# Two of the shared expert's eight groups moved from the prelude to the head of the bridge, normalisation in quarters

## The chip, the cores and the metric

The kernel runs on one core of a Trainium2 chip. Times are device microseconds (us) of one execution. TensorE (PE) multiplies matrices into PSUM, VectorE (DVE), ScalarE (ACT) and GpSimd (POOL) work element by element, SyncE (SP) issues most of the transfers between HBM and SBUF. Everything is float32.

## What is computed

Two layers on 4096 tokens of width 256. Each adds to the stream a mixer and a mixture of experts, both fed by the same layer norm:

```python
xn = _layernorm(x)
x = x + _L0_attn_ref(xn, ...) + _L0_ffn_ref(xn, ...)   # state-space mixer; 16 experts, 4 a token
xn = _layernorm(x)
x = x + _L1_attn_ref(xn, ...) + _L1_ffn_ref(xn, ...)   # linear attention; 8 experts, 2 a token
...
def _L0_ffn_ref(...):
    ...
    shared = _swiglu(x, w1_s, w3_s, w2_s)              # silu(x @ w1.T) * (x @ w3.T) @ w2.T, hidden width 256
    return routed + shared
```

The change is about `shared`, the expert of layer 0 that every token goes through. It needs only layer 0's `xn`, and its result is needed when the stream of layer 0 is complete.

## The kernel before

Tokens come in 32 tiles of 128, and four tiles make a group (`NG` = 8 groups of 512). The program is a row of stages, each a block in which every engine has its own list of instructions; all engines meet between blocks. Within a block they wait for each other through semaphores alone, so the order of a list is what the source writes.

- **Norm phase** (`norm_phase`): loads x in four transfers of eight tiles, computes mean and variance (`moments`) in `PARTS` = 2 halves, ScalarE takes the root (`root`), VectorE writes `xn` of a group and SP stores it to `xn_rows`; TensorE turns it and ScalarE keeps it as `xnT` (column-wise, in SBUF until layer 1 overwrites it group by group). In steps 4 to 7 VectorE waits for the store of the group four before. ScalarE's list also issues the fill `blank` of the 18.6 MB slot buffer, after the second root.
- **Route phase** (`route_phase` with `decay_work` and `Shared`): VectorE computes the mixer's decay (`dt`), then the ranking of experts (`sel`), then, from the count of tokens per expert, the slots. TensorE runs the shared expert in 16 units (`up(j)`: gate and value of half the hidden width of a group) and 8 `down(g)`; before unit `SUMS` = 8 it makes the running sums of `dt` in two halves, and after unit `COUNT` - 1 = 13 the count. ScalarE copies out (`keep_up`, `keep_down`), POOL multiplies, SP stores each group to `shared_rows`. `keep_down(g)` from the third group on waits for the store of the group two before.
- **SSD stage**: the mixer proper, 179 to 1407 us.
- **First expert stage**, with `Join` beside it: per group it loads x, the mixer's output and `shared_rows`, POOL adds the bias, VectorE adds all up in `xs`.
- **Bridge** (`bridge_phase`, layer 1's block): POOL sums each token's four expert rows pairwise (`b_work`, loaded by SP in halves of a group), VectorE adds them to `xs`, normalises a group (one step per group), TensorE turns it and projects q, k and v; then routing and attention. A load for group g + 2 waits for VectorE's add of group g.
- **Second expert stage**, to the end.

## Time and profile before

| | |
|---|---|
| median of 3 runs | 2404.99 us (2403.39 to 2406.26) |
| the profiled execution, its own time | 2406.89 us |
| its span, first to last instruction | 2405.1 us |
| mean granted TensorE clock | 0.969 |
| TensorE busy in the span | 2187.2 us (91%) |
| VectorE, ScalarE, POOL busy | 1595.0, 1190.7, 1435.2 us |
| prelude (norm and route phase) | 0 to 179.3 us |
| SSD stage, first expert stage | 179.3 to 1407.3 to 1693.8 us |
| bridge, second expert stage | 1693.8 to 1963.5 to 2405.1 us |

A busy engine is not one at its peak. What a change is worth is read from the stage in which it sits: who is idle there, and what ended the wait. A granted clock of 1.00 is 2.4 GHz, one of 0.50 is 1.2 GHz.

### The profile page before, as it was taken

How to read it: one execution, taken by the hardware profiler on the slowest of the kernel's cores; microseconds unless marked ns; L12 is line 12 of the kernel's file. 1: busy time of each engine (PE TensorE's matmuls, PEld its weight loads, DVE VectorE, ACT ScalarE, POOL GpSimd, SP SyncE). 2: the span in 40 equal slices, each digit the busy share in tenths (PEclk: the TensorE clock that was granted, in tenths of full speed). 3: DMA queues.
4: the chain of work that ended last, by engine and by line, in shares of the span. 5: the costliest groups of instructions: out<-in, count | busy, mean ns of one | idle time of the engine just before them, and what ended most of it. 6: DMA issues, size and time to landing. Idle time of an engine off the chain costs nothing. (4 is left out here: it accounts for less than half of the span.)

```text
span 2405.1 us, 40728 instructions
## 1 busy us (share of the span) xinstructions
PE 2187.2 (91%) x12292; PEld 1586.7 (66%) x12292; DVE 1595.0 (66%) x3484; ACT 1190.7 (50%) x2677; POOL 1435.2 (60%) x1278
## 2 busy tenths in 40 slices
PE   4787999999999999999999989999288879999997
PEld 2455777777777777777777767777144656666665
DVE  4747888888888888888888845666687742222222
ACT  2356777777777777777777722222132341111111
POOL 1224777777777777777777756777643214444443
PEclk9898999999999999999999999999689899999999
DMA  7926454545545455454544448664540046222221
GB/s 255 359 83 146 139 151 132 152 139 151 149 132 156 136 154 145 133 156 139 153 143 132 141 139 278 191 218 150 202 157 1 1 166 173 46 44 45 45 43 20
DMA packets 195651, 330.34 MB, mean 137 GB/s; under 512 B 49267, under 2 KB 137588, under 8 KB 195188
## 3 DMA queue, kind: packets, MB, share of 16 engines
q1 hardware_dynamic: 139044, 233.43, 32.8%
q0 software_dynamic: 26880, 53.64, 8.8%
q10 hardware_dynamic: 29520, 40.66, 5.4%
q8 instruction: 110, 1.80, 0.3%
q14 instruction: 97, 0.79, 0.1%
HBM read 240.72 MB, written 87.84 MB: 137 GB/s over the span
## 5 line engine op out<-in xcount | busy, mean ns | idle before, releaser
L1006 DVE SCALAR_TENSOR_TENSOR m_cv<-m_hp,conv,m_cv 128x256 f32<-128x256 f32 x864 | 417.0, 483 | 112.2 <-ACT m_cv L905 91.0
L1397 PE MATMUL e_u<-wup,e_xgT 128*128 x1152 | 421.4, 499 | 9.0 <-issue 4.9
L1335 ACT ACTIVATE e_sil<-e_u 128x128 f32<-128x128 f32 (+1 forms) x216 | 82.9, 384 | 551.5 <-PE e_u L1397 524.5
L832 POOL TENSOR_TENSOR m_er<-m_er,m_cT 128x1024 f32<-128x1024 f32 x128 | 302.2, 2361 | 44.1 <-DVE m_ar L1013 44.1
L943 ACT ACTIVATE m_ar<-m_ar,m_ta 128x128 f32<-128x128 f32 x1024 | 318.7, 390 | 0.8
L1094 PE MATMUL m_hp<-xnT,wpj 128*128 128x259 f32 x1152 | 304.3, 387 | 7.8 <-PEq L144 4.5
L1397 PEld LDWEIGHTS e_u<-wup,e_xgT 128*128 128x128 f32 x1152 | 203.1, 191 | 141.3 <-issue 130.3
L1102 PE MATMUL m_gp<-xnT,wpj 128*128 128x256 f32 x1024 | 269.1, 385 | 11.2 <-ACT m_gT L923 11.2
L1094 PEld LDWEIGHTS m_hp<-xnT,wpj 128*128 128x128 f32 x1152 | 214.2, 192 | 68.8 <-issue 27.1
L1292 POOL DMA_INDIRECT out<-e_y,target x72 | 113.0, 1570 | 228.7 <-DVE e_y L1366 192.9
L839 POOL TENSOR_TENSOR m_hdd<-m_hdt,m_tb 128x512 f32<-128x512 f32 x128 | 131.0, 1043 | 193.8 <-DVE m_hdt L1021 193.8
L1153 PE MATMUL m_out<-wo,m_gT 128*128 128x256 f32 x1024 | 242.9, 380 | 0.0
L923 ACT ACTIVATE m_gT<-m_gp,bias 128x256 f32<-128x256 f32 x256 | 121.2, 473 | 232.3 <-PE m_gp L1102 189.2
L1153 PEld LDWEIGHTS m_out<-wo,m_gT 128*128 128x128 f32 x1024 | 193.0, 190 | 47.8 <-issue 23.9
L1414 PE MATMUL e_d<-wdn,e_hidT 128*128 x864 | 222.9, 381 | 1.0 <-DVE e_y L1366 1.0
L1359 DVE SCALAR_TENSOR_TENSOR e_hid<-e_sil,gate,e_u 128x512 f32<-128x512 f32 x72 | 53.8, 747 | 254.6 <-ACT e_sil L1335 240.5
L1102 PEld LDWEIGHTS m_gp<-xnT,wpj 128*128 128x128 f32 x1024 | 178.6, 191 | 35.9 <-ACT m_gT L923 19.1
L1300 POOL DMA_INDIRECT y_rows<-e_y,e_target x144 | 149.4, 1037 | 73.4 <-DVE e_y L1366 64.4
L873 POOL DMA_INDIRECT rows_by_slot<-m_xrow,posi x128 | 172.5, 1347 | 32.8 <-issue 26.5
L905 ACT ACTIVATE m_cv<-m_hp,m_bsum,conv 128x256 f32<-128x256 f32 x288 | 159.9, 555 | 53.9 <-PE m_hp L1094 51.3
L1414 PEld LDWEIGHTS e_d<-wdn,e_hidT 128*128 128x128 f32 x864 | 147.3, 190 | 23.4 <-issue 1.8
L1039 DVE SCALAR_TENSOR_TENSOR m_y<-m_hT,dcol,m_yt 128x128 f32<-128x128 f32 x512 | 143.2, 343 | 23.5 <-PE m_yt L1142 23.5
(305 smaller groups left out, 3965.8 us busy)
## 6 DMA issues: line engine op xcount, KB each, us to landing
m_ar<-acum_rows_dram SPq DMA_DIRECT2D x512, 128.0 KB
m_er<-eacum_rows_dram SPq DMA_DIRECT2D x128, 512.0 KB
rows_by_slot<-blank_rows ACTq DMA_DIRECT2D x1, 18576.0 KB, 79.1
e_xg<-rows_by_slot ACTq DMA_DIRECT2D x132, 129.0 KB
m_xrow<-xn_rows SPq DMA_DIRECT2D x32, 512.0 KB
b_work<-y_rows SPq DMA_DIRECT2D x16, 1024.0 KB, 7.0
wup<-in_w SPq DMA_DIRECT2D x8, 1024.0 KB
wpj<-in_w_proj SPq DMA_DIRECT2D x1, 4352.0 KB, 24.4
```

Source lines behind the costliest of these rows:

```text
L832: g.tensor_tensor(er[:, t], er[:, t], middle(cT[:, t * P:(t + 1) * P], HQ), ALU.mult).then_inc(scaled.sem, 1)
L873: pool.indirect_dma_start(by_slot, bass.IndirectOffsetOnAxis(posi[:, i * TB + t, r:r + 1], 0), xrow[:, t, r, :], None).then_inc(s_scat[t], 16)
L905: a(cv[:, n % 6, :], hp[n % 2][:, OLD:PW], ACT.Identity, bias=bsum[:, c:c + 1], scale=conv[:, c, OLD:TAPS]).then_inc(heva.sem, 1)
L943: ins = a(row, row, ACT.Exp, bias=ta[:, t, q * HQ + h:q * HQ + h + 1])
L1006: v_.scalar_tensor_tensor(o, hp[n % 2][:, j:j + BLK], conv[:, c, j:j + 1], o, ALU.mult, ALU.add).then_inc(tapped.sem, 1)
L1039: ins = v_.scalar_tensor_tensor(y1[:, cols], hT[:, conv_of(cc), t * P:(t + 1) * P], d_col[:, cc:cc + 1], yt[s % 2][:, cols], ALU.mult, ALU ...
L1094: ins = mm(hp[n % 2][:, 0:PW], w_proj[:, kd, col:col + P], xpad[:, kd, ds(i * BLK, PW)], start=kd == 0, stop=kd == KD - 1)
L1102: ins = mm(gp[:, 0:BLK], w_proj[:, kd, cc * P:(cc + 1) * P], xpad[:, kd, ds(i * BLK + OLD, BLK)], start=kd == 0, stop=kd == KD - 1)
L1153: ins = mm(out_ps[:, t * D:(t + 1) * D], gT[:, q % 2 * CQ + c, t * P:(t + 1) * P], w_out[:, cc, :], start=s == 0 and c == 0, stop=cc == CH ...
L1300: pool.indirect_dma_start(y_dram, bass.IndirectOffsetOnAxis(row_of(n), 0), y[:, n % YR, :], None).then_inc(s_y[n % YR], 16)
L1397: ins = nc.tensor.matmul(u_ps[a.slot(2)][b][:, 0:width], xgT[:, a.slot(2), c, :], wup[:, c, ds(e * (2 * f) + b * width, width)], start=c = ...
L1414: ins = nc.tensor.matmul(d_ps[d.slot(2)][:, 0:D], hidT[:, d.slot(2), c * P:(c + 1) * P], wdown[:, ds(e * (FC * D) + c * D, D)], start=c == ...
```

## The change

Four things. `SHARED_EARLY` = 6: the prelude does groups 0 to 5 of the shared expert only. Groups 6 and 7 are computed at the head of the bridge, from layer 0's `xnT`, with the weights loaded once more, in the first expert stage; their results are added to `xs` from PSUM after VectorE's first step. `PARTS` = 4: mean and root by quarters, the second quarter's moments before the first group, the third's before group 2, the fourth's before group 4; the blank fill is issued after the first two roots. `SUMS` = 6 and `COUNT` = 10: the sums stand before unit 6, the count after unit 9. Small buffers of layer 1's routing move into `b_work`.

```diff
+SHARED_EARLY = 6
...
-        PARTS = 2
+        PARTS = 4
...
                 def step(s):
                     if s.inside(NG):
-                        if s.n % (NG // PARTS) == 0:
-                            moments(s.n // (NG // PARTS))
+                        if s.n % 2 == 0:
+                            if s.n // 2 + 1 < PARTS:
+                                moments(s.n // 2 + 1)
+                            invert(s.n // 2)
...
-                    if part == PARTS - 1:
-                        blank(act)
...
-                    if s.inside(NG) and s.n % (NG // PARTS) == 0:
-                        root(s.n // (NG // PARTS))
+                    if s.n in (3, 5):
+                        root((s.n + 1) // 2)
...
+                root(0)
+                root(1)
+                blank(act)
                 pipeline(NG, 2, step)
...
-    UPS = 2 * NG
-    SUMS, COUNT = 8, 14
+    UPS = 2 * SHARED_EARLY
+    SUMS, COUNT = 6, 10
...
-        for g in range(3, NG):
+        for g in range(3, SHARED_EARLY):
             side.store(sp, g)
...
-            for dst, src in zip(at, self.drams):
+            for dst, src in list(zip(at, self.drams))[0:3 if g < SHARED_EARLY else 2]:
...
-            v.tensor_tensor(x, x, self.sr[:, g % 2, u, :], ALU.add).then_inc(self.s_done, 1)
+            v.tensor_tensor(x, x, self.sr[:, g % 2, u, :] if g < SHARED_EARLY else self.b_out[:], ALU.add).then_inc(self.s_done, 1)
...
+                for j in range(2 * len(left)):
+                    g, c = left[j // 2], j % 2
+                    for b, off, done, free in ((f_h1, 0, s_f1, s_fs), (f_h3, FS, s_f3, s_fm)):
+                        if j:
+                            pe.wait_ge(free, j)
+                        for kd in range(KD):
+                            ins = mm(b[:], w13s[:, kd, off + c * P:off + (c + 1) * P], xnT[:, kd, ds(g * GT, GT)],
+                                     start=kd == 0, stop=kd == KD - 1)
+                        ins.then_inc(done, 1)
+                for i in range(len(left)):
+                    pe.wait_ge(s_fm, 2 * i + 2)
...
+                    if s.n == 2:
+                        pe.wait_ge(s_fx, 2 * len(left))
...
+                for j in range(2 * len(left)):
+                    act.wait_ge(s_f1, j + 1)
+                    ac(sil_of(j), f_h1[:], ACT.Silu).then_inc(s_fs, 1)
...
+                for j in range(2 * len(left)):
+                    dve.wait_ge(s_fs, j + 1)
+                    dve.wait_ge(s_f3, j + 1)
+                    v.tensor_tensor(hs_of(j), sil_of(j), f_h3[:], ALU.mult).then_inc(s_fm, 1)
+
+                def add_shared():
+                    for i, g in enumerate(left):
+                        dve.wait_ge(s_fd, i + 1)
+                        for h in range(2):
+                            x = xs[:, g * BIG + 2 * h:g * BIG + 2 * h + 2, :].rearrange("p t d -> p (t d)")
+                            v.tensor_tensor(x, x, f_d[2 * i + h][:], ALU.add).then_inc(s_fx, 1)
...
+                    if s.n == 0:
+                        add_shared()
...
-                     (wsm1[:, :, 0:E1], w_gate1))
+                     (wsm1[:, :, 0:E1], w_gate1), (w13s[:], w13_s), (w2s[:], w2_s))
```

TensorE's list in the route phase, around the sums and the count, before. `f_h` is a unit (a run of x4 is one, x8 two), `f_d` x8 a down, sum and tot the sums, r_within from r_sel the count (it follows further down):

```order
L207 MATMUL f_h<-xnT,w13s 128x512 x8
L217 MATMUL f_d<-w2s,f_hs 128x256 x8
L207 MATMUL f_h<-xnT,w13s 128x512 x4
L633 MATMUL sum<-dt_u,upto 128x512
L634 MATMUL tot<-dt_u,ones 128x512
L637 MATMUL r_within<-upto,dt_u 128x128 x4
L633 MATMUL sum<-dt_u,upto 128x512
L634 MATMUL tot<-dt_u,ones 128x512
L637 MATMUL r_totals<-upto,dt_u 128x128 x4
L207 MATMUL f_h<-xnT,w13s 128x512 x4
L217 MATMUL f_d<-w2s,f_hs 128x256 x8
L207 MATMUL f_h<-xnT,w13s 128x512 x8
```

And after the change:

```order
L208 MATMUL f_h<-xnT,w13s 128x512 x4
L641 MATMUL sum<-dt_u,upto 128x512
L642 MATMUL tot<-dt_u,ones 128x512
L645 MATMUL r_within<-upto,dt_u 128x128 x4
L641 MATMUL sum<-dt_u,upto 128x512
L642 MATMUL tot<-dt_u,ones 128x512
L645 MATMUL r_totals<-upto,dt_u 128x128 x4
L208 MATMUL f_h<-xnT,w13s 128x512 x4
L218 MATMUL f_d<-w2s,f_hs 128x256 x8
L208 MATMUL f_h<-xnT,w13s 128x512 x8
```

The sums stand two units and a down earlier, and between their two halves no unit has come.

ScalarE's list at the same place, with the semaphores that each instruction waits for, before (`f_sil` and `f_h3c` are `keep_up`, `f_shared` is `keep_down`, `tabs` and `dt_z` the copies of the sums):

```order
L226 ACTIVATE f_sil<-f_h 128x512 [waits f_hidden,f_up_gate]
L228 ACTIVATE f_h3c<-f_h 128x512 [waits f_up_value]
L235 ACTIVATE f_shared<-f_d 128x512 [waits f_down,f_shared_stored0]
L235 ACTIVATE f_shared<-f_d 128x512 [waits f_down]
L226 ACTIVATE f_sil<-f_h 128x512 [waits f_hidden,f_up_gate]
L228 ACTIVATE f_h3c<-f_h 128x512 [waits f_up_value]
L606 ACTIVATE tabs<-sum 128x16x32 [waits dt_sums]
L607 ACTIVATE tabs<-tot 128x16x32
L609 ACTIVATE dt_z<-r_within 128x512 [waits dt_rows]
L606 ACTIVATE tabs<-sum 128x16x32 [waits dt_sums]
L607 ACTIVATE tabs<-tot 128x16x32
```

And after:

```order
L614 ACTIVATE tabs<-sum 128x16x32 [waits dt_sums]
L615 ACTIVATE tabs<-tot 128x16x32
L617 ACTIVATE dt_z<-r_within 128x512 [waits dt_rows]
L614 ACTIVATE tabs<-sum 128x16x32 [waits dt_sums]
L615 ACTIVATE tabs<-tot 128x16x32
L617 ACTIVATE dt_z<-r_totals 128x512 [waits dt_rows]
L619 ACT_TABLE_LOAD
L619 ACTIVATE small<-dt_z 128x1024 [waits dt_rows_kept]
L227 ACT_TABLE_LOAD [waits f_hidden]
L227 ACTIVATE f_sil<-f_h 128x512 [waits f_up_gate]
L229 ACTIVATE f_h3c<-f_h 128x512 [waits f_up_value]
L236 ACTIVATE f_shared<-f_d 128x512 [waits f_down,f_shared_stored0]
```

The first instruction that waits for `f_shared_stored0` stood ahead of the copies of the sums, and now stands behind them.

VectorE's list at the head of the bridge, before (`b_work` the expert rows, `b_xn` the normalised group):

```order
L1801 TENSOR_TENSOR xs<-xs,b_work 128x1024 [waits b_y_summed]
...
L1817 RECIPROCAL b_rstd<-b_tmp 128x4 [waits b_row_std,b_row_moments]
L1823 TENSOR_SCALAR b_xn<-xs,b_mean,b_rstd 128x256 [waits b_row_rstd]
L1823 TENSOR_SCALAR b_xn<-xs,b_mean,b_rstd 128x256 x3
L1801 TENSOR_TENSOR xs<-xs,b_work 128x1024 [waits b_y_summed]
```

And after (`b_raw<-b_raw,b_bank` are the products of the hidden halves, `xs<-xs,b_bank` the adds of the shared result):

```order
L1835 TENSOR_TENSOR b_raw<-b_raw,b_bank 128x512 [waits b_shared_value,b_shared_silu] x4
L1855 TENSOR_TENSOR xs<-xs,b_work 128x1024 [waits b_y_summed]
...
L1871 RECIPROCAL b_rstd<-b_tmp 128x4 [waits b_row_std,b_row_moments]
L1877 TENSOR_SCALAR b_xn<-xs,b_mean,b_rstd 128x256 [waits n0_small_kept]
L1877 TENSOR_SCALAR b_xn<-xs,b_mean,b_rstd 128x256 x3
L1842 TENSOR_TENSOR xs<-xs,b_bank 128x512 [waits b_shared_down]
L1842 TENSOR_TENSOR xs<-xs,b_bank 128x512
L1842 TENSOR_TENSOR xs<-xs,b_bank 128x512 [waits b_shared_down]
L1842 TENSOR_TENSOR xs<-xs,b_bank 128x512
```

Four products stand ahead of the first add, and four adds behind the first normalised group.

## Rows read from the trace of the kernel before

**Rows 1.** Route phase by stretch: length, busy PE, PEld, DVE, ACT, POOL; PEclk, DMA share, GB/s.
```profile
67.90:179.30 111.40, 94.79 (x284) 54.12 (x284) 71.55 (x118) 49.55 (x81) 23.50 (x21) 0.93 0.62 212
```

**Rows 2.** Timeline, TensorE: start, length, line, instructions, idle time before, its releaser.
```profile
68.03 13.48 PE L207 MATMUL f_h<-xnT,w13s 128*128 128x512 f32 x24 [4.17 <-PEq L144]
...
121.67 2.08 PE L633 MATMUL sum<-dt_u,upto 128*128 128x512 f32 x2 [10.03 <-ACT tabs L607]
143.16 7.03 PE L207 MATMUL f_h<-xnT,w13s 128*128 128x512 f32 x16
150.03 3.62 PE L217 MATMUL f_d<-w2s,f_hs 128*128 128x256 f32 x16
156.92 1.02 PE L457 MATMUL r_within<-r_sel,before 128*128 128x512 f32 x2
179.37 1.98 PE L1094 MATMUL m_hp<-xnT,wpj 128*128 128x259 f32 x4 [4.50 <-PEq L144]
```

**Rows 3.** Timeline, ScalarE in the route phase.
```profile
118.57 1.08 ACT L235 ACTIVATE f_shared<-f_d 128x512 f32<-128x512 f32 x2 [15.79 <-DMA shared_rows<-f_shared]
```

**Rows 4.** Landing times: the first shared store; the blank fill (DMA issues of the page).
```profile
DMA to landing us min/median/max: 19.5/19.5/19.5
...
rows_by_slot<-blank_rows ACTq DMA_DIRECT2D x1, 18576.0 KB, 79.1
```

**Rows 5.** Timeline, VectorE in the route phase.
```profile
98.20 1.23 DVE L590 SCALAR_TENSOR_TENSOR dt_u<-dt,exp_a 128x1024 f32<-128x1024 f32 x1
123.06 0.43 DVE L509 TENSOR_SCALAR r_sel<-r_rank 128x512 f32<-128x512 f32 x1
158.91 1.89 DVE L522 TENSOR_TENSOR_SCAN r_incl<-ones,r_totals 128x32 f32<-128x32 f32 x16 [31.16 <-PE r_totals L458]
```

**Rows 6.** Norm phase: timelines of VectorE and TensorE; xn stores (all, fifth) and landings.
```profile
18.55 0.18 DVE L302 TENSOR_TENSOR n_mean<-n_stats 128x16 f32<-128x16 f32 x1
20.66 5.34 DVE L321 TENSOR_SCALAR n_xn<-xs,n_mean,n_rstd 128x256 f32<-128x256 f32 x16
...
40.44 1.06 PE L377 MATMUL n_t<-ident,n_xn 128*128 128x128 f32 x8 [2.22 <-DVE n_xn L321]
54.03 1.09 PE L377 MATMUL n_t<-ident,n_xn 128*128 128x128 f32 x8 [1.29 <-ACT xnT L360]
...
L287 SPq DMA_DIRECT2D xn_rows<-n_xn x8: 359/360/381, 22.1 to 50.1; - x8
DMA to landing us min/median/max: 5.1/8.8/20.2
...
L287 SPq DMA_DIRECT2D xn_rows<-n_xn x1: 359/359/359, 40.3 to 40.3; - x1
DMA to landing us min/median/max: 12.4/12.4/12.4
```

**Rows 7.** Busy time by stretch, as in rows 1: VectorE's first three steps of the bridge.
```profile
1706.10:1722.80 16.70, 0.00 (x0) 0.00 (x0) 15.98 (x17) 0.20 (x1) 15.96 (x15) 0.50 0.34 126
1722.80:1728.70 5.90, 1.97 (x8) 1.57 (x8) 5.24 (x18) 1.18 (x3) 0.00 (x0) 0.50 0.83 267
1728.70:1745.10 16.40, 10.39 (x28) 5.41 (x28) 15.75 (x18) 3.13 (x7) 14.42 (x8) 0.81 0.57 225
```

**Rows 8.** VectorE's first step; POOL's pair sums and their loads; m_state (ns min/median/max).
```profile
1706.16 1.22 DVE L1801 TENSOR_TENSOR xs<-xs,b_work 128x1024 f32<-128x1024 f32 x1 [19.66 <-POOL b_work L1613]
...
L1611 POOL TENSOR_TENSOR b_work<-b_work x16: 2332/2343/2396, 1698.8 to 1780.9; 128x1024 f32<-128x1024 f32 x16
L1613 POOL TENSOR_TENSOR b_work<-b_work x16: 1262/1267/2146, 1701.2 to 1783.3; 128x512 f32<-128x512 f32 x16
DMA to landing us min/median/max: 4.9/7.0/11.1
...
L1031 DVE TENSOR_TENSOR m_state<-m_state,m_up x128: 673/678/689, 213.6 to 1403.6; 128x512 f32<-128x512 f32 x128
```

**Rows 9.** TensorE's unit matmuls (L207) alone, by stretch: the granted clock.
```profile
74.00:76.00 2.00, 2.00 (x6) 0.86 (x5) 1.00 0.93 253
```

More of the change, by code:

```diff
@@ L294, in moments @@
                 def moments(part):
-                    for n in range(part * 2, part * 2 + 2):
-                        dve.wait_ge(s_x[n], 16)
-                        for t in range(n * T // 4, (n + 1) * T // 4):
-                            nc.vector.bn_stats(stats[:, t, :], xs[:, t, :]).then_inc(s_stats, 1)
+                    dve.wait_ge(s_x[part], 16)
+                    for t in range(part * T // PARTS, (part + 1) * T // PARTS):
+                        nc.vector.bn_stats(stats[:, t, :], xs[:, t, :]).then_inc(s_stats, 1)
                     dve.wait_ge(s_stats, (part + 1) * T // PARTS)
@@ L1464, in add_bias @@
         g, rest = divmod(n - self.FIRST + 4, 11)
-        if rest or not 0 <= g < NG:
+        if rest or not 0 <= g < SHARED_EARLY:
             return
@@ L1517, in bridge_phase @@
         vv, weff, mask = sb("vv", [P, KD, P]), sb("weff", [P, KD, D]), sb("mask", [P, P])
-        sel, wgt, rank, pos, rt, incl = (sb(n, [P, T, e_n]) for n in ("sel", "wgt", "rank", "pos", "rtmp", "incl"))
         cmp = work[:, 0:T * e_n * e_n].rearrange("p (t a b) -> p t a b", a=e_n, b=e_n)
+        sel, wgt, rank, pos, rt, incl = (work[:, 2048 + n * T * e_n:2048 + (n + 1) * T * e_n].rearrange("p (t e) -> p t e", e=e_n)
+                                         for n in range(6))
         row = sb("row", [P, T])
@@ L1542, in bridge_phase @@
         at_unit = lambda n: bank[4 + n % 4]
+        left = range(SHARED_EARLY, NG)
+        block_of = lambda n: raw[:, n % 4, ds((NG - 1 - n // 4) * GT, GT)]
+        sil_of, hs_of = (lambda j: block_of(j)), (lambda j: block_of(4 + j))
+        f_h1, f_h3, f_d = bank[4], bank[5], (bank[6], bank[7], bank[2], bank[3])
+        s_f1, s_f3, s_fs, s_fm, s_fd, s_fx = (sem("b_" + n) for n in (
+            "shared_gate", "shared_value", "shared_silu", "shared_hidden", "shared_down", "shared_added"))
         plane = lambda r, g: raw[:, r, ds(g * GT, GT)] if r < R - KD else xnT[:, r - (R - KD), ds(g * GT, GT)]
@@ L1649, in unit @@
                     ins.then_inc(s_pj, 1)
+                for j in range(2 * len(left)):
[9 more added lines that the diff above has]
+                    pe.wait_ge(s_fm, 2 * i + 2)
+                    for u in range(BIG):
+                        for c in range(FS // P):
+                            ins = mm(f_d[2 * i + u // 2][:, u % 2 * D:(u % 2 + 1) * D], hs_of(2 * i + c)[:, u * P:(u + 1) * P],
+                                     w2s[:, c, :], start=c == 0, stop=c == FS // P - 1)
+                    ins.then_inc(s_fd, 1)
                 def step(s):
                     a = s.back(1)
+                    if s.n == 2:
+                        pe.wait_ge(s_fx, 2 * len(left))
                     if a.inside(NG):
@@ L2046, in program @@
         with Semaphores(nc, sem) as own:
-            bridge_phase(nc, own, k, xs, y0, xnT, rows, wsm1, wqkv, wp, g_sb, b_sb, bp_sb, lists1, etab1, etabs[1], out, s_out)
+            bridge_phase(nc, own, k, xs, y0, xnT, rows, wsm1, wqkv, wp, g_sb, b_sb, bp_sb, lists1, etab1, etabs[1], out, s_out, w13s, w2s)
         with ExitStack() as e:
```

17 lines of the change are left out of this document (13 added, 4 removed).

## The prediction

> **What bounds the kernel now.** The stages first [rows 1]. TensorE is all but full in the SSD stage and in both expert stages, which the change leaves alone; the slack is in the prelude (in its route phase TensorE is busy for 94.8 of 111.4 us, VectorE for 71.6) and in the bridge.
>
> Then TensorE in the route phase [rows 2]. It runs units (two matmul groups each: a pair takes 6.87 us, 143.16 to 150.03) and downs (3.45 us), with one hole, 10.03 us before the second half of the sums. The count starts at 156.92, and from it to the SSD stage's first matmul (179.37) are 22.45 us. Why the hole: ScalarE sat 15.79 us before `keep_down(2)`, for the store of group 0's shared rows [rows 3], which took 19.5 us to land [rows 4]. That wait stands ahead of the sums' copies in ScalarE's order, so TensorE's second half of the sums waits with it. VectorE has `sel` at 123.5, has nothing left from 127.75 on (158.91 less its wait), and waits 31.16 us for the count [rows 5]. So the prelude is a chain through TensorE with ScalarE's store wait in it; VectorE is the next bound, close behind.
>
> In the norm phase [rows 6] VectorE's first group starts at 20.66, and TensorE takes groups 4 to 7 at 40.44 to 54.03, 4.5 us apart. In the bridge [rows 7] VectorE works in eight steps, one a group: the first three take 16.7, 5.9 and 16.4 us, and long and short alternate after that. The long ones are those in which POOL is busy with pair sums (15.96 of 16.70 us, against 0.00 of 5.90). The first starts at 1706.16, after 19.66 us without work, 12.3 us into the stage [rows 8].
>
> **The route phase, step by step.** Ahead of the count four units and two downs go: 2 x 6.87 + 2 x 3.45 = 20.6 us. The sums move ahead of `keep_down(2)`: the 10.03 us become two short waits, one for `dt_u` (ready at 98.20 + 1.23 = 99.43 [rows 5], where unit 5 ended at some 98.5), one for ScalarE's two copies between the halves, 1.1 us by the pair of copies in [rows 3]. That is 2.0, so 8.0 us are gained. The second half took 4.3 us right after the hole (121.67 to 125.9) at the low clock; with hardly a pause before it, 2.8: 1.5 more. Together 30.1 us before the count. Behind it the order stays (two units, two downs): 22.45 us.
>
> What has to keep up. `keep_down(2)` comes some 113 us after the start, and group 0's store must have landed by then. Before, it landed at 118.6, behind the blank fill (79.1 us to landing [rows 4]), which now goes out some 16 us earlier. I put the landing midway between 102.6 and 118.6, at 110: no wait; the upper end is a wait of 5 us. VectorE: `sel` at 123.5 precedes the count at 156.9 - 30.1 = 126.8, and its own floor for the SSD stage's first matmul is 127.75 + (179.37 - 158.91) = 148.2, against 126.8 + 22.45 = 149.25 by the count. So at most 1 us more is to be had there, and a late TensorE costs at once. ScalarE's and SP's last pieces follow the last down as before; SP's row stores start earlier by what the sums do.
>
> **The norm phase.** With quarters VectorE does the same sixteen statistics before its first group, and one chain of seven small ops more (18.55 to 20.05, 1.5 us), part of it in a short wait for x: the first group is 1.1 us later. Behind it groups 2 and 3 wait for eight statistics and another chain, groups 4 and 5 no longer for the second root. Between 1.1 (the start alone) and 1.8 (what group 2 loses) I take 1.2.
>
> A second price: the fill is now issued at 21.5, ahead of the xn stores, and VectorE waits at groups 4 to 7 for stores 0 to 3 to land. Without the fill a store landed in 5.1 us; with it the fifth, out at 40.3, in 12.4, the last, out at 50.1, in 20.2: at 52.7 and 70.3, 5.9 us apart [rows 6]. Store 0 goes out at 23.0, 1.5 us behind the fill: landed at 35.4, or at 40 with the weights ahead of it. Then 41 to 46, 47 to 52, 53 to 58. VectorE had group 7 ready 3.9 us before TensorE took it (50.1, 54.03), so the stores must land by some 40, 45, 49 and 54: nothing to 4 us, and I take 1.5. Norm phase: +2.7 us.
>
> By the Trainium skill (DMA: Bandwidth & Descriptors, "Queues, rings and completion order") each DMA engine takes turns between its queues, a packet each. If that meant equal shares, stores would move as fast as the fill's 18576 KB in 79.1 us, 2.2 us for 512 KB, nothing would wait, and the norm phase would cost 1.2 us for 2.7. The landings 5.9 us apart are against equal shares.
>
> Prelude: 30.1 - 2.7 = 27.4 us less, the SSD stage at about 152.
>
> **SSD and first expert stage.** Two of POOL's bias sums and two loads go; two weight loads (768 KB) come in SP's queue behind group 1's. TensorE is the full engine there and neither queue feeds it at those places: nothing. With that cover gone, one load of the size would be at most 7.0 us, as those of [rows 8].
>
> **The bridge.** TensorE's four units start at 1693.9, after a pause. In the route phase, after a like pause, three took 13.48 us [rows 2], 3.2 over the full clock's price: the granted clock was back at 1.00 by 74 [rows 9]. So 13.48 + 3.44 = 16.9 us, to 1710.8, and VectorE's last product ends 0.9 later (0.68 for 128x512 with one operand in PSUM [rows 8]), at 1711.7. SiLU is the table that ScalarE has loaded; Sqrt's load moves behind it and still has 5 us. VectorE's first step begins 5.5 us late. The downs (6.9 us) end by 1717.7, and four adds of 0.68, 2.7 us, follow the first step. Sum 8.2 us if nothing hides them.
>
> What hides them: POOL goes on meanwhile. A group's pair sums take it 7.3 us [rows 8] (2.34, and 1.27 for each second op), and group 1's ran under VectorE's first step; half are done when it now starts. The step's own work is 5.9 us (the step without POOL), so it ends near 1718.4, with the adds near 1721.1, where it ended at 1722.8. But group 2's sums are fed by that step's first add, through a load of 7.0 us: they run at 1720 to 1727.5, now under step 1, which was free. It will take 8 to 10 us for 5.9 and end near 1730 for 1728.7. After that long and short go on as before. I take +2 us, between -3 (all hidden, fewer sums left to collide with) and +8.2.
>
> Here the skill has a rule that speaks against the change (SBUF — State Buffer, "Who interferes with whom"): VectorE and GpSimd have a pair of ports in common, and one blocks the other for a whole instruction. The long and short steps agree. By it each op of step 1 that meets POOL pays up to 2.34 us; the new products and adds, with one input in PSUM, pay nothing, which m_state's 673 to 689 ns over 128 bear out.
>
> **The sum.** -27.4 + 2 = -25.4 us. The profiled execution took 2406.89 (2405.1 and 1.8 around it): 2381.5. The median of the runs, 2404.99, is 1.9 lower: 2379.6.
>
> **Rivals.**
> 1. Landings: the stores hold the norm phase up by 4 us, or group 0's store holds ScalarE by 5, or both: up to 7.5 more than I took, 2383 to 2387. For it: 12.4 to 20.2 us. Against: the middle of each estimate meets its deadline. 15%.
> 2. The bridge hides nothing: all four units run at the low clock, 27.5 us for 16.9, and VectorE starts 16.1 late; with the adds 18.8, less what fewer collisions give back, +12 to +19: 2389 to 2397. For it: the granted clock was 0.50 in VectorE's first two steps, 0.81 in the third [rows 7]. Against: TensorE had next to no work there, while in the route phase the clock rose in the first two units. 9%. (TensorE: Matmul & The Clock Gate, "What's actually happening", in the Trainium skill has sustained work lift the clock: by that, the trace agrees, 16.9.)
> 3. Slower: the late start shifts the beat so that POOL's sums fall under the four short steps too. At 16.5 us each for some 6 to 8 they would add up to 38 us: 2417. It decides from 27 us on. Against: POOL has eight groups of 7.3 us in all and one and a half are done before VectorE starts, so the long steps shrink by what the short ones take. 3%.
> 4. The gain isn't there: VectorE's chain, next to POOL's products and with no slack left, sets the prelude's end, and the change does not shorten it: within 0.2% of before. It would need 25 us where VectorE now idles for 31.16. 2%.
> My forecast has the rest, 71%, from 2371 (no stall in the norm phase, -1.5; two waits of the sums gone, -2; -3 for +2 in the bridge) to 2388.
>
> A measurement of this kernel tells 0.2% (4.8 us) from no change. Faster 0.94, same 0.02, slower 0.04 (rival 3 and a little for what I don't see). The range, 2371 to 2391, takes in rival 1 and leaves most of rival 2.
>
> **What the changed profile would show.** The sums' second half at 103 to 109 with under 2 us of wait; no wait for a store before `keep_down(2)`; the count at 128 to 131; VectorE's wait before r_incl under 3 us for 31.16; the SSD stage's first matmul at 150 to 154. In the bridge VectorE's first add 17.5 to 19 us into the stage (before 12.3), the second 26 to 29 (before 29), and the stage 0 to 4 us longer. I am wrong if ScalarE still waits for group 0's store, if xn groups 4 to 7 wait over 4 us for stores, or if the four units take over 20 us.

## The result

The changed kernel takes 2381.22 us (median of 4 runs, 2380.25 to 2383.89), the kernel before 2405.62 on the same chip (4 runs): ratio 0.9898, 95% interval 0.9881 to 0.9915. The prediction was 2379.6. A later repeat (c_changed below) gave 2381.44 and 2409.15, ratio 0.9887 (0.9868 to 0.9905). The span of the profiled execution went from 2405.1 to 2378.5 us. By stages, from TensorE's rows (the bridge is counted from the end of TensorE's last `e_d` of the first expert stage, 1686.04 before, to its first instruction in the second, 1969.90 before):

| stage | before | after | difference | predicted |
|---|---|---|---|---|
| to TensorE's first unit (norm phase) | 68.03 | 68.04 | 0.0 | +2.7 |
| from there to the SSD stage's first matmul | 111.3 | 80.5 | -30.8 | -30.1 |
| SSD and first expert stage | 1506.7 | 1506.5 | -0.2 | 0 |
| bridge | 283.9 | 288.3 | +4.5 | +2 |
| second expert stage, to the end | 435.2 | 435.1 | -0.1 | 0 |

The profile after, TensorE in the route phase, where [rows 2] stood (timeline: start, length, line, instructions, in brackets the idle time before and what ended it):

```profile
99.53 1.13 PE L641 MATMUL sum<-dt_u,upto 128*128 128x512 f32 x2 [0.81 <-DVEq L599]
102.69 1.13 PE L641 MATMUL sum<-dt_u,upto 128*128 128x512 f32 x2 [0.28 <-ACT tabs L615]
126.06 1.02 PE L465 MATMUL r_within<-r_sel,before 128*128 128x512 f32 x2
...
140.29 3.72 PE L218 MATMUL f_d<-w2s,f_hs 128*128 128x256 f32 x16 [2.03 <-POOL f_hs L244]
148.53 2.99 PE L1102 MATMUL m_hp<-xnT,wpj 128*128 128x259 f32 x8 [4.52 <-PEq L145]
```

The hole of 10.03 us is gone: the sums wait 0.81 us for `dt_u` and 0.28 us for the copies. The count starts at 126.06 for 156.92, and from it to the SSD stage's first matmul are 22.47 us, as before.

ScalarE's first `keep_down` that waits for a store, and the landing times of group 0's store and of the fill (those of [rows 3] and [rows 4]):

```profile
110.94 0.60 ACT L236 ACTIVATE f_shared<-f_d 128x512 f32<-128x512 f32 x1
```

```profile
DMA to landing us min/median/max: 7.3/7.3/7.3
...
rows_by_slot<-blank_rows ACTq DMA_DIRECT2D x1, 18576.0 KB, 81.7
```

No bracket: nothing was waited for. The fill, issued at 20.6, has landed at 102.3, ahead of group 0's store, which goes out at 98.5 and takes 7.3 us for 19.5.

VectorE, to set beside [rows 5]:

```profile
122.19 0.43 DVE L517 TENSOR_SCALAR r_sel<-r_rank 128x512 f32<-128x512 f32 x1
128.05 1.89 DVE L530 TENSOR_TENSOR_SCAN r_incl<-ones,r_totals 128x32 f32<-128x32 f32 x16 [1.20 <-PE r_totals L466]
...
147.18 0.17 DVE L550 TENSOR_SCALAR etab_i<-r_ef 128x2 int32<-128x2 f32 x1
```

It waits 1.20 us for the count where it waited 31.16, and its last route instruction ends 1.2 us ahead of the SSD stage. So VectorE has next to no slack left in this phase either.

The norm phase, VectorE's groups and then TensorE's with the xn stores, for [rows 6]:

```profile
20.86 2.67 DVE L328 TENSOR_SCALAR n_xn<-xs,n_mean,n_rstd 128x256 f32<-128x256 f32 x8
45.29 1.67 DVE L328 TENSOR_SCALAR n_xn<-xs,n_mean,n_rstd 128x256 f32<-128x256 f32 x4 [1.12 <-DMA xn_rows<-n_xn]
50.55 1.38 DVE L328 TENSOR_SCALAR n_xn<-xs,n_mean,n_rstd 128x256 f32<-128x256 f32 x4 [1.93 <-DMA xn_rows<-n_xn]
```

```profile
54.05 1.09 PE L385 MATMUL n_t<-ident,n_xn 128*128 128x128 f32 x8 [1.29 <-ACT xnT L365]
68.04 2.90 PE L208 MATMUL f_h<-xnT,w13s 128*128 128x512 f32 x3 [4.17 <-PEq L145]
...
L288 SPq DMA_DIRECT2D xn_rows<-n_xn x8: 359/360/464, 22.3 to 52.0; - x8
DMA to landing us min/median/max: 11.5/19.7/22.8
```

With the fill ahead of them the stores land in 11.5 to 22.8 us for 5.1 to 20.2, and VectorE does wait for two of them, 1.12 and 1.93 us. TensorE notices neither: it takes group 7 at 54.05 for 54.03.

The bridge: TensorE's four units, then picked lines of VectorE (its last product, the adds that open its steps, the four shared adds, two small operations of the second step), for the first row of [rows 8]:

```profile
1663.24 16.48 PE L1675 MATMUL b_bank<-xnT,w13s_again 128*128 128x512 f32 x32 [8.19 <-PEq L145]
...
1679.83 0.69 DVE L1835 TENSOR_TENSOR b_raw<-b_raw,b_bank 128x512 f32<-128x512 f32 x1 [2.75 <-PE b_bank L1675]
1680.43 3.29 DVE L1855 TENSOR_TENSOR xs<-xs,b_work 128x1024 f32<-128x1024 f32 x1
...
1688.42 2.47 DVE L1842 TENSOR_TENSOR xs<-xs,b_bank 128x512 f32<-128x512 f32 x4
1690.81 1.28 DVE L1855 TENSOR_TENSOR xs<-xs,b_work 128x1024 f32<-128x1024 f32 x1
...
1693.57 1.97 DVE L1863 TENSOR_TENSOR b_mean<-b_lstats 128x4 f32<-128x4 f32 x1
...
1697.11 2.28 DVE L1867 TENSOR_TENSOR b_var<-b_lstats 128x4 f32<-128x4 f32 x1
...
1705.07 1.21 DVE L1855 TENSOR_TENSOR xs<-xs,b_work 128x1024 f32<-128x1024 f32 x1
...
1710.97 1.22 DVE L1855 TENSOR_TENSOR xs<-xs,b_work 128x1024 f32<-128x1024 f32 x1
```

Four units took 16.48 us (16.9 forecast), the first add starts 17.2 us behind the first of them (1680.43 - 1663.24). Counted alike in both kernels, from the end of the first expert stage's last `e_d`, it starts at +25.4 for +20.1. Then the second step, short before the change (5.90 us in [rows 7]), takes 14.26 us (1690.81 to 1705.07), and the third is the short one. Two of its operations on 4 elements a lane show why: 1.97 and 2.28 us for 0.17. POOL in the same stretch (the last of group 1's sums, the first of group 2, of group 3 and of group 4):

```profile
1682.72 2.13 POOL L1631 TENSOR_TENSOR b_work<-b_work 128x512 f32<-128x512 f32 x1
1688.64 2.36 POOL L1629 TENSOR_TENSOR b_work<-b_work 128x1024 f32<-128x1024 f32 x1 [3.79 <-DMA b_work<-y_rows]
...
1697.03 2.34 POOL L1629 TENSOR_TENSOR b_work<-b_work 128x1024 f32<-128x1024 f32 x1 [0.18 <-DMA b_work<-y_rows]
...
1714.15 2.37 POOL L1629 TENSOR_TENSOR b_work<-b_work 128x1024 f32<-128x1024 f32 x1 [9.80 <-DMA b_work<-y_rows]
```

and in the kernel before, the same place (the last of group 1's sums, the first of group 2, the first of group 3):

```profile
1713.85 1.27 POOL L1613 TENSOR_TENSOR b_work<-b_work 128x512 f32<-128x512 f32 x1
1715.08 2.33 POOL L1611 TENSOR_TENSOR b_work<-b_work 128x1024 f32<-128x1024 f32 x1
1730.00 2.35 POOL L1611 TENSOR_TENSOR b_work<-b_work 128x1024 f32<-128x1024 f32 x1 [7.57 <-DMA b_work<-y_rows]
```

Before, POOL went from group 1 to group 2 without a pause, and took three groups in one run, the last two of them under VectorE's first step. Now it stands still for 3.79 us until group 2's rows have landed. Then it takes groups 2 and 3 in one run with 0.18 us between them (group 3's load, released by VectorE's second step at 1690.81, has landed by 1697.03), and all of it lies under that second step.

### The profile page after: what moved, and what is told of

The parts are those of the page before. It is cut to its first block and busy times, and to the rows that moved or that the text cites. A ratio compares the mean times of both kernels' runs of the same rounds, so it can differ in the third digit from the quotient of the medians.

```text
span 2378.5 us, 40732 instructions
## 1 busy us (share of the span) xinstructions
PE 2186.9 (92%) x12292; PEld 1587.3 (67%) x12292; DVE 1596.0 (67%) x3508; ACT 1187.8 (50%) x2671; POOL 1425.0 (60%) x1272
## 5 line engine op out<-in xcount | busy, mean ns | idle before, releaser
L913 ACT ACTIVATE m_cv<-m_hp,m_bsum,conv 128x256 f32<-128x256 f32 x288 | 160.5, 557 | 54.9 <-PE m_hp L1102 49.9
```

Source lines behind the costliest of these rows:

```text
L913: a(cv[:, n % 6, :], hp[n % 2][:, OLD:PW], ACT.Identity, bias=bsum[:, c:c + 1], scale=conv[:, c, OLD:TAPS]).then_inc(heva.sem, 1)
```

## The experiments

Each is the changed kernel with one edit. The table gives for all of them TensorE's count and the SSD stage's first matmul (from the start), then, counted from the end of TensorE's last `e_d`, VectorE's first add, TensorE's transposes of the last group and the length of the bridge, and the median time (in brackets where there is a single run). The sets differ: the kernel before took 2395.7, 2409.2, 2407.7 and 2397.6 us in the four, and the first expert stage alone, which no edit here is aimed at, took 266 to 275 us. So the columns are compared across sets, the times only within one.

| kernel | set | count | first matmul | first add | last transposes | bridge | time |
|---|---|---|---|---|---|---|---|
| before | - | 156.92 | 179.37 | +20.1 | +111.3 | 283.9 | |
| changed | - | 126.06 | 148.53 | +25.4 | +116.5 | 288.3 | |
| c_changed | 2 | 125.91 | 148.36 | +25.6 | +117.1 | 288.4 | 2381.4 |
| e1_none_moved | 1 | 126.31 | 169.40 | +20.2 | +111.2 | 284.0 | 2390.0 |
| e8_one_moved | 3 | 126.10 | 158.87 | +20.4 | +112.1 | 284.8 | 2387.3 |
| e2_blank_late | 1 | 127.81 | 151.95 | +25.3 | +116.9 | 287.8 | (2377.1) |
| e3_sums_late | 1 | 125.40 | 149.87 | +25.3 | +116.7 | 288.1 | (2375.0) |
| e9_move_alone | 3 | 134.67 | 157.12 | +25.3 | +116.6 | 288.0 | 2389.4 |
| e4_left_out | 1 | 126.17 | 148.62 | +20.4 | +110.9 | 281.5 | (2370.1) |
| e5_no_adds | 2 | 125.66 | 148.14 | +25.4 | +113.1 | 285.1 | (2379.5) |
| e10_adds_inside | 3 | 126.51 | 148.99 | +25.6 | +116.9 | 288.7 | (2384.3) |
| e6_interleaved | 2 | 126.56 | 149.04 | +21.9 | +113.9 | 284.9 | 2380.8 |
| e7_sums_held | 2 | 126.70 | 150.86 | +25.5 | +118.4 | 288.6 | 2386.4 |
| e11_on_time | 4 | 125.70 | 148.16 | +20.5 | +121.3 | 292.8 | 2377.5 |

### What the move is worth in the prelude

```diff
-SHARED_EARLY = 6
+SHARED_EARLY = 8
```

> The changed kernel with all eight groups of the shared expert in the prelude; sums before unit 6, count after unit 9, quarters and the early fill stay. Theory A (the move is worth TensorE's work behind the count, less what it costs in the bridge): the count stays at 126 to 127 and VectorE ends at 147 to 148, but TensorE has four units and two downs more behind the count (20.6 us), so the SSD stage's first matmul is at 169 (148.53 after the change), and the bridge goes back to its length of before, some 4.4 us shorter. Total 2381.2 + 20.6 - 4.4 = 2397. Theory B (VectorE's chain set the prelude's end, the move brought nothing there): first matmul at 149 to 152, total 2377 to 2380.

```profile
169.40 2.93 PE L1102 MATMUL m_hp<-xnT,wpj 128*128 128x259 f32 x6 [4.50 <-PEq L145]
```

First matmul at 169.40, where 169 was expected; the bridge is back to 284.0. Ratio to the kernel before 0.9973 (0.9961 to 0.9985), which is 18 us above the changed kernel's 0.9898, for the 16.2 of theory A. So the count is early without the move: it stands behind unit 9 instead of unit 13 (four units and two downs, 20.6 us), and the wait before the sums is gone. Neither shortens what TensorE has to do: without the move the units stand behind the count, and the prelude ends only 10.0 us earlier than before, about the old hole. The move takes them away from there, 20.9 us. No run takes back the place of the count or the quarters alone.

```diff
-SHARED_EARLY = 6
+SHARED_EARLY = 7
...
-            sp.wait_ge(self.s_st[n], SHARED_EARLY // 2 * 16)
+            sp.wait_ge(self.s_st[n], (SHARED_EARLY - n + 1) // 2 * 16)
```

> The changed kernel with one group moved (group 7) instead of two; seven groups in the prelude. Theory A (behind the count TensorE's work is the bound, and in the bridge only a late VectorE costs): two units and a down more behind the count, the SSD stage's first matmul at 159 (148.5 + 10.3); in the bridge the last product ends before POOL's first two sums are there, so VectorE's first add comes at +20 to +21 us, and step 1 is short again, step 2 long; two adds instead of four; the last transposes at +111 to +113, the bridge 284 to 286. Total 5 to 8 us over the changed kernel. Theory B (the units in the bridge cost by themselves, late or not): the bridge 286 to 287, total 8 to 9 over.

```profile
158.87 3.24 PE L1102 MATMUL m_hp<-xnT,wpj 128*128 128x259 f32 x8 [4.50 <-PEq L145]
...
1685.59 1.23 DVE L1855 TENSOR_TENSOR xs<-xs,b_work 128x1024 f32<-128x1024 f32 x1 [1.97 <-POOL b_work L1631]
1703.46 1.21 DVE L1855 TENSOR_TENSOR xs<-xs,b_work 128x1024 f32<-128x1024 f32 x1
1709.36 1.22 DVE L1855 TENSOR_TENSOR xs<-xs,b_work 128x1024 f32<-128x1024 f32 x1
```

First matmul at 158.87 (159 expected). VectorE starts on time, its second step is short again (1703.46 to 1709.36, 5.9 us), the bridge takes 284.8. Its ratio is 0.9909 (0.9892 to 0.9927). One group is worth 10.5 us in the prelude and costs 0.9 in the bridge; the second is worth 10.3 and costs 3.5.

### The fill and the sums

```diff
+                    if s.n == 4:
+                        blank(act)
...
                 root(1)
-                blank(act)
```

> The changed kernel with the blank fill issued where it was before, at step 4 of the norm phase, some 16 us later. Theory A (the early fill is what freed group 0's store): the fill lands at 117 to 120, the store of group 0 with it, ScalarE waits 6 to 9 us before keep_down(2), which now stands behind the copies of the sums; TensorE gets a hole of 4 to 7 us behind the sums, the count comes at 131 to 134, first matmul of the SSD stage at 153 to 156, total 2386 to 2389. Theory B (the new order of the sums alone took the wait off the path): the wait is there on ScalarE, the count stays at 126 to 128, total within 2 us of 2381. In the norm phase the xn stores land in 5 to 20 us as before and VectorE's two waits for them (1.12 and 1.93) are gone, with nothing gained in the phase's length.

ScalarE's `keep_down(2)`:

```profile
115.75 1.09 ACT L236 ACTIVATE f_shared<-f_d 128x512 f32<-128x512 f32 x2 [4.35 <-DMA shared_rows<-f_shared]
```

The wait is back, 4.35 us for the 6 to 9 expected (the fill took 74.5 us here), behind the sums. The count comes at 127.81, 1.8 us later, which is theory B's range (126 to 128) and not A's (131 to 134); the first matmul comes 3.4 us later. The xn stores land in 4.4 us (median) for 19.7 and VectorE's waits for them are gone, and TensorE takes group 7 no earlier (54.40 for 54.05).

```diff
-    SUMS, COUNT = 6, 10
+    SUMS, COUNT = 8, 10
```

> The changed kernel with the sums before unit 8, as before, and the count after unit 9. Theory A (with the fill early the place of the sums does not matter, since ScalarE has no store to wait for): no store wait over 2 us, the second half of the sums at 112 to 115 with under 2 us of idle time, the count at 125 to 127, first matmul at 147 to 151, total within 2 us of 2381. Theory B (the place of the sums removed the hole): a hole of 6 to 10 us before their second half, the count 5 us or more later, total 2386 or more.

```profile
112.36 1.12 PE L641 MATMUL sum<-dt_u,upto 128*128 128x512 f32 x2 [0.28 <-ACT tabs L615]
125.40 1.02 PE L465 MATMUL r_within<-r_sel,before 128*128 128x512 f32 x2
149.87 2.50 PE L1102 MATMUL m_hp<-xnT,wpj 128*128 128x259 f32 x5 [4.50 <-PEq L145]
```

With the fill early the place of the sums does not matter: 0.28 us before the second half, the count 0.7 us earlier than in the changed kernel. The first matmul is 1.3 us later for another reason, which e7_sums_held shows.

Both edits together:

> The changed kernel with the fill at its place of before and the sums before unit 8, so of the prelude's changes the two moved groups, the quarters and the count after unit 9 are left. Theory A (either the early fill or the early sums frees the sums of the store wait; without both it is back): ScalarE waits 8 to 14 us for group 0's store before keep_down(2), TensorE has a hole of 3 to 9 us before the second half of the sums, the count at 130 to 135, first matmul of the SSD stage at 153 to 158, total 2386 to 2391 where the changed kernel has 2381. Theory B (the wait only fills time in which VectorE has not got its ranking anyway, since the count cannot be before 123): the count at 126 to 128, first matmul at 148 to 151, total as the changed kernel.

```profile
116.46 1.09 ACT L236 ACTIVATE f_shared<-f_d 128x512 f32<-128x512 f32 x2 [13.03 <-DMA shared_rows<-f_shared]
```

```profile
119.56 2.08 PE L642 MATMUL sum<-dt_u,upto 128*128 128x512 f32 x2 [7.27 <-ACT tabs L616]
134.67 1.02 PE L466 MATMUL r_within<-r_sel,before 128*128 128x512 f32 x2
157.12 3.02 PE L1103 MATMUL m_hp<-xnT,wpj 128*128 128x259 f32 x8 [4.50 <-PEq L145]
```

The old picture: 13.03 us on ScalarE, a hole of 7.27 us, the count at 134.67, first matmul at 157.12, 8.6 us later than in the changed kernel. The ratio is 0.992 (0.9903 to 0.9938). So either of the two frees the sums. At the count, the fill taken back alone costs 1.8 us, the sums alone nothing, and both 8.6. All of it is as theory A has it.

### What the bridge pays for

Units, products, downs and adds left out:

```diff
-        left = range(SHARED_EARLY, NG)
+        left = range(0)
```

> The changed kernel without the two groups' work in the bridge: units, products, downs and adds left out, so layer 0's shared expert is missing for the last two groups of tokens; the two weight loads stay. Theory A (the bridge's 4.4 us come from VectorE's late start and the adds): VectorE's first add 12 to 12.5 us into the stage, second step short (6 us) and third long (16 us) as before the change, the bridge 4 to 5 us shorter than in the changed kernel, total 2376 to 2378. Theory B (they come from elsewhere, as the buffers of the routing that moved into b_work, or the later loads): the bridge stays at 4 us over before, total 2380 or more.

The bridge takes 281.5 us, 6.9 less than in the changed kernel, and the last transposes come 5.6 us earlier. VectorE starts at +20.4, and long and short steps stand as before the change. So the 4.5 us come from the two groups' work, and not from the buffers in `b_work` or the loads. That the bridge is 2.4 us shorter than before lies mostly behind the last transposes (170.6 us for 172.6). The bridge of e1_none_moved has the same list and takes 284.0, 172.8 of them behind its last transposes, so the 2.4 us are not of the program; they may be of the data, which are wrong here for two groups, or spread. Against e1_none_moved the work costs 4.3 us.

The adds alone left out:

```diff
-                    if s.n == 0:
-                        add_shared()
...
```

The two waits for these adds, TensorE's and VectorE's, go with them.

> The changed kernel without the four adds of the shared result (units, products and downs stay; layer 0's shared expert is missing for the last two groups of tokens). Theory A (the late start of VectorE's first step shifts the beat: POOL's sums of groups 2 and 3 now lie under step 1, and those of 6 and 7 under step 5, and the adds only fill time that step 1 would spend blocked): second step starts 2.5 us earlier and ends within 1 us of where it ended, the last group's transposes stay at +115.5 to +116.5 us. Theory B (the adds are on the path with their 2.5 us): the last transposes at +114 and the bridge 2.5 us shorter.

Neither theory holds. The second step starts 2.4 us earlier and ends where it did, within 0.7 us, as A has it; and the bridge is 3.4 us shorter, as B has it. The gain comes later, in the fourth step, which takes 15.5 us for 19.6 (adds at +55.3 and +70.7, for +55.8 and +75.4): POOL had a pause of 1.23 us there just before VectorE came to its four scalings, but on the same set 3.6 of the 4.1 us were already gained when the scalings began (9.2 us into the step for 12.8 in c_changed), in the chain of small operations beside POOL's sums. In the six profiles that have the changed kernel's list up to this step it takes 18.1 to 19.6 us, so 15.5 is outside what changes by itself; where in the meeting of the two engines the gain arises is not shown.

The adds behind the first add of step 1, under POOL's sums:

```diff
-                    if s.n == 0:
-                        add_shared()
...
                         v.tensor_tensor(xs[:, at, :], xs[:, at, :], yg[:, s.n % 2, :, 0, :], ALU.add).then_inc(s_x, 1)
+                        if s.n == 1:
+                            add_shared()
```

> The changed kernel with the four adds of the shared result behind the first add of step 1 instead of behind step 0, so under POOL's sums of groups 2 and 3, which do not slow an add that reads PSUM. Theory A (the adds cost because they stand in POOL's pause and push step 1 back): the second step starts at +33.2 us for +35.6, each shared add still takes 0.6 us, step 1 ends where it did (+49.5 to +50.5), the third step's add likewise, and the last transposes come anywhere between +113 and +117 depending on where POOL's next sums meet step 3. Theory B: the adds cost 2.5 us wherever they stand: step 1 ends at +50 and the bridge is the same within 1 us.

VectorE and POOL at the start of step 1:

```profile
1691.99 1.22 DVE L1855 TENSOR_TENSOR xs<-xs,b_work 128x1024 f32<-128x1024 f32 x1
1693.13 2.47 DVE L1842 TENSOR_TENSOR xs<-xs,b_bank 128x512 f32<-128x512 f32 x4
...
1692.23 3.19 POOL L1629 TENSOR_TENSOR b_work<-b_work 128x1024 f32<-128x1024 f32 x1 [3.81 <-DMA b_work<-y_rows]
```

Four adds took 2.47 us under POOL's sums. In the changed kernel they took 2.47 us too, and there, other than the expectation has it, they also ran under a sum nearly from their start (1688.42, the sum from 1688.64). In e11_on_time they stand in a real pause of POOL (1699.81 us, no sum between 1698.77 and 1708.33) and took 2.46 us. So an add with one operand in PSUM is not slowed. Step 1 again ends at +49.8, and nothing is gained. That lies within both theories, so the run does not tell them apart. With e5_no_adds beside it, where step 1 ends at +49.4 without any adds, the adds cost nothing within that step, and what their absence gained came two steps later.

VectorE's first step ahead of the fourth product, the second down behind group 0's transposes, the adds behind step 1:

```diff
...
-                for j in range(2 * len(left)):
+                def product(j):
...
+                for j in range(3):
+                    product(j)
...
                     if s.n == 0:
+                        product(3)
+                    if s.n == 1:
                         add_shared()
```

> The changed kernel with VectorE's first step between the third and the fourth product, the second down behind group 0's transposes, and the adds behind step 1. VectorE's first add comes at +22 us for +25. Theory A (POOL's beat sets the bridge: a load and two groups of sums for two steps): the first step grows under POOL's sums, the second too, and the last transposes come 1 to 3 us earlier (+113.5 to +115.5); total 1 to 3 us under the changed kernel. Theory B (work on VectorE sets it): the last transposes stay at +116 to +117, since as much work as before is done.

VectorE's first add, and POOL's last sum of group 1 and first of group 2:

```profile
1678.07 2.90 DVE L1860 TENSOR_TENSOR xs<-xs,b_work 128x1024 f32<-128x1024 f32 x1
...
1684.49 1.27 POOL L1631 TENSOR_TENSOR b_work<-b_work 128x512 f32<-128x512 f32 x1
1686.07 2.34 POOL L1629 TENSOR_TENSOR b_work<-b_work 128x1024 f32<-128x1024 f32 x1 [0.31 <-DMA b_work<-y_rows]
```

The first add comes 3.6 us earlier, and that is enough: group 2's rows are there 0.31 us after group 1's sums, three groups go in one run as before the change, the second step ends at +46.6 for +49.9, and the last transposes come at +113.9, as theory A has it. The bridge is 3.5 us shorter. The time, 2380.8 for 2381.4 on the same chip, does not tell the two apart: this profile's prelude and SSD stage were 1.7 us longer, and the 1 to 3 us of theory A were not measured.

POOL's sums of group 6 held back until VectorE has ended step 5:

```diff
+                    if h == 12:
+                        pool.wait_ge(s_xn, 6)
```

> The changed kernel with one wait more: POOL starts the pair sums of group 6 only when VectorE has ended step 5. Theory A (step 5 is long, 17 us for 6, only because POOL's sums of groups 6 and 7 lie under it, and its end sets TensorE's last three groups): step 5 takes 6 to 8 us, group 5's transposes at +89 to +91 for +98, group 6 and 7 wait for the held sums instead: the last transposes at +112 to +114 for +116.5, total 2 to 4 us under the changed kernel. Theory B (holding POOL only moves the wait): the last transposes at +116 or later, total the same or more.

```profile
1747.83 2.36 POOL L1631 TENSOR_TENSOR b_work<-b_work 128x1024 f32<-128x1024 f32 x1 [16.20 <-DVE b_xn L1879]
```

POOL stands for 16.20 us. Step 5 is then short (its transposes at +90.3 for +99.1), as A has it, but step 6 has to wait for the sums pushed back, and of the 8.8 us its transposes keep 0.9 (+108.0 for +108.9); the last transposes come at +118.4, the bridge takes 288.6. B holds: holding POOL moves the wait. The time is 5 us over the changed kernel's, with intervals that overlap (ratio 0.9905, 0.9886 to 0.9925, for 0.9887, 0.9868 to 0.9905), and of that the bridge accounts for 0.1 in the profiles; 2.5 lie in the prelude and 2.7 in the SSD stage, where the programs are the same. In its profile the last down of the prelude takes 5.41 us for 3.72, after the same pause of 2.03 us; below it the granted clock of 141 to 145 us:

```profile
140.93 5.41 PE L218 MATMUL f_d<-w2s,f_hs 128*128 128x256 f32 x16 [2.03 <-POOL f_hs L244]
...
141.00:145.00 4.00, 4.00 (x11) 3.23 (x12) 3.83 (x6) 0.42 (x1) 0.00 (x0) 0.57 0.03 11
```

In the changed kernel's first profile the clock in the same stretch was 1.00 (2.4 GHz, against 0.57 here, mostly the lower level of 1.2 GHz):

```profile
141.00:145.00 4.00, 3.01 (x14) 2.30 (x13) 3.83 (x6) 1.53 (x3) 0.00 (x0) 1.00 0.01 4
```

ScalarE's last copy and exponential follow that down, and the SSD stage starts 2.5 us later. The same 5.41 us stand in e2_blank_late and e3_sums_late: it explains the 1.3 us of the one and about half of the 3.4 of the other.

Two products ahead of the first step, one behind it, one inside step 1:

```diff
...
-                for j in range(2 * len(left)):
+                def product(j):
...
+                for j in range(2):
+                    product(j)
...
                         ins.then_inc(s_lst, 1)
+                        if s.n == 1:
+                            product(3)
...
                     if s.n == 0:
+                        product(2)
+                    if s.n == 1:
                         add_shared()
```

TensorE makes the fourth unit and the second down behind group 0's transposes.

> The changed kernel with only two products ahead of VectorE's first step, the third behind it, the fourth inside step 1 and the adds behind step 1; TensorE makes the fourth unit and the second down behind group 0's transposes. All of the two groups' work is done, but VectorE's first step starts when POOL's first sums are there. Theory A (the late start shifts the beat, the work itself hides in VectorE's short steps): first add at +20.4 us, step 0 long (16 to 17 us), step 1 short (7 to 8 us), long steps the even ones as before the change, the last transposes at +112 to +114, the bridge 284 to 286 us, total 1 to 4 us under the changed kernel, that is 24 to 29 us under the kernel before. Theory B (the work on VectorE costs its own time wherever it stands): the last transposes at +116 to +117 and the bridge at 288.

VectorE inside step 1:

```profile
1690.55 0.69 DVE L1845 TENSOR_TENSOR b_raw<-b_raw,b_bank 128x512 f32<-128x512 f32 x1 [3.66 <-PE b_bank L1675]
```

VectorE started at +20.5, POOL took three groups in one run, and still the bridge is the longest of all, 292.8 us. The second step waits 3.66 us for TensorE's fourth unit, which comes only behind group 0's transposes and takes 4.91 us, at a granted clock of 0.73 after 12.04 us of waiting, for the 3.60 of a unit at the full clock, and so the step is still under way when POOL's next run begins (1691.43): 18.0 us for 5.9. Both theories missed: an early start is worth nothing if a short step is stretched into the next run. Its ratio to the kernel before is 0.992 (0.9906 to 0.9933), where the changed kernel has 0.9898 and 0.9887.

The changed kernel once more, beside these:

> The changed kernel itself, as the measure for the others on this chip. Bridge as in its first profile: from TensorE's last e_d to the second expert stage's first matmul 288 us (before the change 284), VectorE's adds at +25, +36, +50, +56, +75 us, the last group's transposes at +116.5.

It came as expected, within 0.6 us in every column.

## Why the prediction was right, and where it was not

The time was met to 1.6 us, with luck in it. Two misses cancel in part: the prelude gave 30.8 us for 27.4, and the bridge took 4.5 for 2, so the span fell by 26.6 us for 25.4. And the forecast took 1.9 us off for the median of the runs against the profiled execution, where the changed kernel's median lies 1.0 above it (2381.22, 2380.25): a spread of executions, which nothing in the forecast explains.

**Route phase, right.** Four units and two downs less ahead of the count, the hole down to two short waits (2.0 us forecast, 1.09 measured), the second half of the sums shorter (102.69 to 105.41, 2.7 us for 4.3): 30.1 forecast, 30.9 measured for the count. Nothing moved behind it (22.45 and 22.47). VectorE's floor was met too: it waits 1.20 us. e1_none_moved and e8_one_moved show the move's part to 0.3 us. What the prediction did not see is that the order of the sums and the early fill do the same thing: it credited the 8.0 us to the sums, and e3_sums_late shows that with the early fill the sums may stay where they were. Group 0's store was put at 110, and landed at 105.8.

**Norm phase, a term mis-sized.** 2.7 us were taken, 0.0 came: so the count was put at 128 to 131 and the first matmul at 150 to 154, and they came at 126.06 and 148.53. "The first group is 1.1 us later" failed: it came 0.2 later (20.86 for 20.66), as the extra chain of 1.4 us fell where VectorE had waited 0.30 us for x and 0.36 for the root, and the first statistics began 0.5 us earlier (12.27 for 12.80). The stall for stores was there, 3.05 us, within the nothing to 4 given; but VectorE was far enough ahead for TensorE to see none of it. The Trainium skill has each DMA engine take turns between its queues, a packet each (DMA: Bandwidth & Descriptors, "Queues, rings and completion order"). Had that meant equal shares, the stores would have landed beside the fill in 2.2 us, by the estimate in the prediction; they took 11.5 to 22.8. The trace speaks against equal shares of bytes; it cannot say anything on turns by packet.

**The bridge, where the step failed.** The 4.5 us were still inside the bounds given (-3 to +8.2), but outside the 0 to 4 us that were named as its sign. Up to VectorE's first add all was as forecast: 16.48 us for the units, the first add 17.2 us in (forecast 17.5 to 19), 5.3 us late for 5.5. "It will take 8 to 10 us for 5.9" and "After that long and short go on as before" are what failed: step 1 took 14.3 us, and from there the odd steps are the long ones, 1, 3 and 5, where it was 0, 2, 4 and 6. That group 2's sums would run under step 1, after a pause of POOL, was right (4.9 us forecast, 3.79 measured). What was missed is what such a pause does to group 3. The load of group 2 waits for the first add, and its rows are there 8.0 to 8.2 us after that add begins (1678.07 to 1686.07 in e6_interleaved, 1680.43 to 1688.64 in the changed kernel). Before, group 1's sums ended 9.0 us after it (1706.16 to 1715.1), so POOL took three groups in a run, and group 3's load was released only when that run was over (1722.83). Now group 1's sums end 4.4 us after the add (1684.85), POOL stops, group 2's sums begin 2.2 us before VectorE's second step, and that step's add (1690.81) releases group 3's load early enough for its rows to be there when group 2 is summed. So two groups of sums, 1688.64 to 1704.35, and not one fall under step 1, and it ends at 1705.07. TensorE, which has 8.2 us of work a group, takes its last groups from the end of the last long step: group 5's transposes at +98.2 for +93.6. Rival 3 has the first half of this right: the late start does shift the beat. The second half, sums under the short steps too, did not come: the long steps moved and did not become more, as its own counterargument says. That the late start is the switch is shown by e8_one_moved and e6_interleaved, which keep half of the work or all of it and start earlier, against c_changed. It is not the whole: e5_no_adds is 3.4 us shorter with the late start and e11_on_time 4.4 us longer without it, so where a later run of sums meets a step counts as much. The split of the 4.5 us between the two is open.

The Trainium skill has VectorE and GpSimd block each other for a whole instruction where both need the shared ports (SBUF — State Buffer, "Who interferes with whom"). The trace agrees: operations of 0.17 us took up to 2.28 beside POOL's sums of 2.35 us, and the products and shared adds, with one operand in PSUM, took 0.69 and 0.62 us beside such sums. Operations with a single tensor to read in SBUF were held as well: VectorE's four scalings took 3.85 us in step 1 and 6.96 in step 3, for 1.38.

Rival 1 did not come (no wait for group 0's store), nor rival 2 (the units ran at 16.48 us, not 27.5), nor rival 4. For the SSD and first expert stage the nothing forecast came (-0.2 us); the 7.0 us given there as the most that a load could cost is the median of [rows 8], whose landings go up to 11.1.

## What to carry to other kernels

When two engines wait in turn for the same stretch, count the work ahead of the joint and behind it apart. The two groups moved away were worth their full length here, and left the other engine 1.2 us of slack; by that a third would have been worth little, which no run tests. Two cures for one wait do not add: take each back alone and both together before crediting either. And where a producer on one engine runs in bursts that slow its consumer, a late start is not priced by its length but by whether the next loads still land within the burst: here 5.3 us of lateness took group 2's sums out of the first burst and put them, with group 3's, under the step that had been free.

## What the hardware showed that was not expected

- In kernels with the same prelude (the changed kernel, e7_sums_held) the last down of the route phase took 3.72 or 5.41 us, after the same idle time of 2.03 us, with the granted clock at 1.00 or 0.57 in the stretch. That is 1.7 us on the path by the clock alone.
- POOL is held as well: its sum of 128x1024 took 3.19 us for 2.35 where VectorE's add had begun 0.24 us before it.
- The first expert stage, nearly the same in all kernels here, took 266 us in set 4, 267 to 268 in set 1 and 271 to 275 elsewhere. That is half or more of the difference between the sets.
